# The last batch of a fused recurrence and mixture-of-experts kernel: both experts in token halves, with the gate and the output behind the second halves

## What is computed

```python
s0, s1, s2 = [_dense(x, share_wi[i], share_wo[i]) for i in range(3)]   # relu(x @ wi) @ wo, 256 -> 1024 -> 256
out_a = relu(x @ expert_wi[t]) @ expert_wo[t]         # t = type_idx of the batch
out_b = relu(x @ expert_wi[t + 1]) @ expert_wo[t + 1]
expert_out = out_a * wa + out_b * wb                  # wa, wb: softmax(gate_vecs / 0.1) of the type
gi = concatenate([expert_out[:, 0], s0[:, 0], s1[:, 0], s2[:, 0]])     # token 0 alone
g = softmax(relu(gi @ gate_w1) @ gate_w2)
out = expert_out * g[0] + s0 * g[1] + s1 * g[2] + s2 * g[3]
```

## Time and profile before

| | |
|---|---|
| median of 3 runs | 1095.56 us |
| the profiled execution's own time | 1094.21 us |
| its span, first to last instruction | 1092.3 us |
| TensorE busy | 98% of the span |
| VectorE busy | 70% |
| ScalarE busy | 37% |
| last matmul of the mixture starts | 1078.84 us |
| mean granted clock of TensorE | 0.998 of full speed |

### The profile page before, as it was taken

How to read it: one execution, slowest core, us unless ns; L and a number is a source line. 1 busy time by engine, 2 the same in 40 slices (tenths; PEclk the granted TensorE clock), 3 DMA queues, 4 the chain that set the end, 5 groups by cost and what they waited for, 6 DMA issues and landing times.

```text
span 1092.3 us, 12453 instructions
## 1 busy us (share of the span) xinstructions
PE 1074.0 (98%) x4754; PEld 862.7 (79%) x4754; DVE 764.0 (70%) x1245; ACT 398.9 (37%) x628; POOL 8.9 (1%) x20
## 2 busy tenths in 40 slices
PE   7899999999999999999999999999999999999998
PEld 5488777788887888878887888878888788888886
DVE  7979987499654995469753896549955598544234
ACT  6454445422334234332344223433234323322221
POOL 0000000000000000000000000000000000000000
PEclk9999999999999999999999999999999999999999
DMA  6359888676444564546544564545645465446550
GB/s 220 109 206 380 304 331 305 235 292 239 155 161 166 209 240 151 191 149 256 176 155 156 208 248 160 193 155 193 235 152 192 155 245 198 147 164 218 185 193 19
DMA packets 36476, 219.58 MB, mean 201 GB/s; under 512 B 4354, under 2 KB 4610, under 8 KB 14786
## 3 DMA queue, kind: packets, MB, share of 16 engines
q1 hardware_dynamic: 34114, 206.22, 52.4%
q0 software_dynamic: 2304, 12.58, 3.0%
HBM read 185.10 MB, written 33.69 MB: 200 GB/s over the span
## 4 chain that ended last, share of the span: by engine, by line
PE 87%; DVE 10%; issue 1%; ACT 1%; DMA 1%; SPq 0%; DVEq 0%
PE ps_up L581 13%; PE ps_up L582 13%; PE ps_up L583 13%; PE ps_down L582 12%; PE ps_down L583 12%; PE ps_down L581 12%; PE ps_aux L581 3%; PE ps_aux L583 3%; PE ps_aux L582 3%; DVE trace L1160 1%; DVE hid_lo L1063 1%; DVE trace L1191 1%; DVE wi L1055 1%; PE ps_aux L709 1%; DVE temporal L1200 1%
## 5 line engine op out<-in xcount | busy, mean ns | idle before, releaser
L1063 DVE SCALAR_TENSOR_TENSOR hid_lo<-ps_up,hid_hi 128x512 fp32r<-128x512 f32 x320 | 218.4, 685 | 272.5 <-ACT hid_hi L861 270.8
L861 ACT ACTIVATE hid_hi<-ps_up 128x512 fp32r<-128x512 f32 x320 | 191.2, 597 | 552.3 <-PE ps_up L583 551.7
L581 PE MATMUL ps_up<-x_hi_all,wi 128*128 128x512 f32 (+1 forms) x644 | 256.2, 398 | 0.1
L583 PE MATMUL ps_up<-x_hi_all,wi 128*128 128x512 f32 (+1 forms) x644 | 253.8, 394 | 0.0
L582 PE MATMUL ps_up<-x_lo_all,wi 128*128 128x512 f32 (+1 forms) x644 | 253.2, 393 | 0.0
L581 PE MATMUL ps_down<-hid_hi,wo 128*128 128x512 f32 x640 | 250.8, 392 | 1.4 <-DVE hid_lo L1063 1.0
L583 PE MATMUL ps_down<-hid_hi,wo 128*128 128x512 f32 x640 | 251.7, 393 | 0.0
L582 PE MATMUL ps_down<-hid_lo,wo 128*128 128x512 f32 x640 | 251.7, 393 | 0.0
L581 PEld LDWEIGHTS ps_down<-hid_hi,wo 128*128 128x128 f32 x640 | 120.2, 188 | 30.9 <-issue 2.6
L583 PEld LDWEIGHTS ps_up<-x_hi_all,wi 128*128 128x128 f32 x644 | 120.9, 188 | 29.1
L581 PEld LDWEIGHTS ps_up<-x_hi_all,wi 128*128 128x128 f32 x644 | 121.7, 189 | 27.6 <-DVE x_lo_all L1055 0.3
(11 more groups left out here) (202 smaller groups left out, 837.4 us busy)
## 6 DMA issues: line engine op xcount, KB each, us to landing
wi<-split_wi SPq DMA_DIRECT2D x70, 1024.0 KB, 4.8
wo<-split_wo SPq DMA_DIRECT2D x70, 1024.0 KB, 4.9
modb<-mod_scratch SPq DMA_DIRECT2D x28, 512.0 KB, 4.4
split_wi<-wi SPq DMA_DIRECT2D x10, 1024.0 KB, 6.6
split_wo<-wo SPq DMA_DIRECT2D x10, 1024.0 KB, 8.7
xt<-in_x SPq DMA_DIRECT2D x8, 512.0 KB, 6.3
split_wi<-ex POOLq DMA_DIRECT2D x4, 1024.0 KB, 7.9
split_wo<-ex POOLq DMA_DIRECT2D x4, 1024.0 KB, 6.6
```

Source lines behind the costliest of these rows:

```text
L581: pe.matmul(ps, w_hi, x_hi, start=start, stop=False)
L583: return pe.matmul(ps, w_lo, x_hi, start=False, stop=stop)
L861: act.activation(hid_hi[:, k % NU, :], ps_up[k % NU][:, :], ACT.Relu).then_inc(hid_hi_ready, 1)
L1063: dve.scalar_tensor_tensor(hid_lo[:, k % NU, :], ps_up[k % NU][:, :], 0.0, f32(hid_hi[:, k % NU, :]), ALU.max, ALU.subtract).then_inc(hid_ ...
```

## The change

In the last batch the slots of the two experts are split in token halves, in the order a, b, b, a: slots 24 to 31 are expert a on tokens 0 to 255, 32 to 39 expert b on the same, 40 to 47 expert b on tokens 256 to 511, 48 to 55 expert a on these. Expert b's weights stay in their buffers for 40 to 47; expert a's are loaded a second time, by eight DMAs of 512 KB that SyncE issues at slots 33, 34, 35 and 37, into tensors that the last batch no longer needs. Second-half expert b adds up in `ps_aux[1]`. A plan of its own, LAST_PLANS, places the gate and the mixing of this batch beside slots 40 to 55: the half-0 expert sum and the gate from slot 40 on, the mixing of half 0 at 44.5 to 46, the three shared terms of half 1 at 47.5 to 49.5, expert b at 50.5 and expert a behind slot 55, with one multiplication of VectorE each that reads the bank itself. Half 0 is stored at 47, half 1 at the end. The fillers and the diagonal matmuls are gone. The rows of `x2_hi`, `x2_lo`, `xg_hi` and `xg_lo` began 8, 16, 24 or 32 bytes behind the start of their tensor's 64-byte blocks, because of an edge of 2 elements ahead of each row; now they begin at multiples of 64 bytes (EDGE 2 becomes 16, and in `x2_hi` and `x2_lo` only the view that is read at an edge keeps one).

```diff
+LAST_PLANS = {
+    "sync": {47: ["store0"], 55.5: ["store1"]}, "tensor": {41.5: ["gate_hidden"]}, "scalar": {43: ["gate_exp"]},
+    "vector": {40: ["gate_part"], 42: ["gate_logits"], 43.5: ["gate_soft", "final_scale"],
+               44.5: ["final_early0"], 45: ["final_early1"], 45.5: ["final_early2"], 46: ["final_early3"],
+               47.5: ["final_late0"], 48.5: ["final_late1"], 49.5: ["final_late2"], 50.5: ["final_expert_b"],
+               55.5: ["final_expert_a"]}, "gpsimd": {},
+}
-EDGE = 2
-FINAL_OWN = P
+LAST_PASSES = ((0, slice(0, T)), (1, slice(0, T)), (2, slice(0, T)), (3, slice(0, HALF)), (4, slice(0, HALF)),
+               (4, slice(HALF, T)), (3, slice(HALF, T)))
+LAST_SLOTS = len(LAST_PASSES) * TPF
+AGAIN = LAST_SLOTS - TPF
+EDGE = 16
...
-        x2_hi_all = sb("x2_hi_all", [P, 2, CT, EDGE + T], F32R)
+        x2_hi_all = sb("x2_hi_all", [P, 2 * CT * T + CT * EDGE], F32R)
...
-                for k in range(SLOTS):
+                for k in range(LAST_SLOTS if last else SLOTS):
+                    if k == SLOTS:
+                        p = ending
...
+        again_wi = [(xg_hi, xg_lo), (ct_hi[:, :, :], ct_lo[:, :, :])]
+        again_wo = [(wc_hi[:, 0:UT * E], wc_lo[:, 0:UT * E]),
+                    tuple(t[:, 0, :, :].rearrange("p c t -> p (c t)") for t in (x2_hi, x2_lo))]
...
+                if last and k in (33, 34):
+                    load_again_wi(k - 33)
+                if last and k in (35, 37):
+                    load_again_wo((k - 35) // 2)
+                if last and k >= SLOTS:
+                    return
...
+                elif step in ("store0", "store1"):
+                    h = int(step[-1])
+                    sp.wait_ge(final_mixed[h], (NS + 1 + h) * CT)
+                    sp.dma_start(out[f].rearrange("p (c t) -> p c t", c=CT)[:, :, half(h)], x2[:, p.f_parity, :, half(h)])\
+                        .then_inc(last_stored[h], 16)
...
+                if j == 0 and at >= AGAIN:
+                    pe.wait_ge(again_loaded[u % 2], 64)
...
+                    if at == AGAIN:
+                        pe.wait_ge(experts_ready, b * 2 + 1 + c)
+                    start, stop = k % TPF == 0, k % TPF == TPF - 1
+                    bank = ps_down[c][:, tokens]
+                    if SLOTS <= at < AGAIN:
+                        bank = ps_aux[1][:, c * HALF:(c + 1) * HALF]
+                        start, stop = start and c == 0, stop and c == CT - 1
...
-            fill("mix", ps_aux[1])
-            pe.wait_ge(experts_ready, B * 2)
-            for at, i in enumerate(MIX_ORDER):
-                pe.wait_ge(final_diag, at + 1)
-                mm = pe.matmul(ps_aux[1][:, FINAL_OWN:T], final_gates[:, i * P:(i + 1) * P],
-                               y[:, y_at(i, (B - 1) % 2), 1, FINAL_OWN:T], start=(at == 0), stop=(at == 3))
-            mm.then_inc(final_sum, 1)
...
+            def final_add(h, at, parity, part, scale):
+
+                for c in range(CT):
+                    if at:
+                        dve.wait_ge(final_mixed[h], 2 * at - 1 + c)
+                    dve.scalar_tensor_tensor(x2[:, parity, c, half(h)], part(c), scale, x2[:, parity, c, half(h)],
+                                             ALU.mult, ALU.add).then_inc(final_mixed[h], 1)
...
+                elif step == "final_expert_a":
+                    dve.wait_ge(down_done, (B - 1) * SLOTS + LAST_SLOTS)
+                    final_add(1, NS + 1, parity, lambda c: ps_down[c][:, half(1)], final_w[:, 0:1])
...
                 elif step == "gate_part":
                     if final(f):
-                        dve.wait_ge(first_token, 2)
-                    else:
-                        dve.wait_ge(experts_ready, f * 2 + 2)
+                        add_expert_b(f, half(0), experts_ready)
+                    dve.wait_ge(experts_ready, f * 2 + 2)
```

More of the change, by code:

```diff
@@ L374, in drive, with run @@
         def drive(eng, mixture, beside):
-            def alone(p, slots):
-                for k in slots:
-                    for s in [*p.steps(eng, k), *p.steps(eng, k + 0.5)]:
-                        beside(s, k, p)
-            def run(b, parity, p, last):
-                for k in range(SLOTS):
+            def run(b, parity, p, last, ending=None):
+                for k in range(LAST_SLOTS if last else SLOTS):
+                    if k == SLOTS:
+                        p = ending
                     for s in p.steps(eng, k):
@@ L396, in drive, with slot_of @@
             last = Period(None, B - 2, None, 0, [first.uses[m] + (B - 2) * uses[m] for m in range(2)])
-            run(B - 1, 1, last, True)
-            yield "mixture ends"
             after = [first.uses[m] + (B - 2) * uses[m] + last.uses[m] for m in range(2)]
-            alone(Period(None, B - 1, None, 1, after), range(SLOTS))
+            run(B - 1, 1, last, True, Period(None, B - 1, None, 1, after, LAST_PLANS))
+        def slot_of(k, last):
+            if last:
+                ffn, tokens = LAST_PASSES[k // TPF]
+                return ffn * TPF + k % TPF, tokens
+            return k, slice(0, T)
+        again_wi = [(xg_hi, xg_lo), (ct_hi[:, :, :], ct_lo[:, :, :])]
+        again_wo = [(wc_hi[:, 0:UT * E], wc_lo[:, 0:UT * E]),
+                    tuple(t[:, 0, :, :].rearrange("p c t -> p (c t)") for t in (x2_hi, x2_lo))]
         block = ctx.enter_context(nc.Block())
@@ L486, in load_wo, with load_again_wi, load_again_wo @@
                 sp.dma_start(f32(wo[:, buf, :, :]).rearrange("p s f -> p (s f)"), source).then_inc(wo_landed[buf], 16)
+            def load_again_wi(half):
+                source = split_wi[bass.ds(expert["now"] + NS, 1), half].rearrange("o p (s c f) -> (o p) s c f", s=2, c=CT)
+                for part, place in enumerate(again_wi[half]):
+                    sp.dma_start(f32(place), source[:, part, :, :]).then_inc(again_loaded[half], 16)
+            def load_again_wo(half):
+                source = split_wo[bass.ds(expert["now"] + NS, 1), half].rearrange("o p (s f) -> (o p) s f", s=2)
+                for part, place in enumerate(again_wo[half]):
+                    sp.dma_start(f32(place), source[:, part, :]).then_inc(again_loaded[half], 16)
             def load_x(m):
@@ L569, in _ @@
             load_raw_wo(2)
-            for _ in drive("sync", mixture, beside):
-                pass
+            drive("sync", mixture, beside)
             sp.wait_ge(out_stored, (B - 1) * 16)
-            for c in range(CT):
-                sp.wait_ge(last_stored[c], 16)
+            for h in range(2):
+                sp.wait_ge(last_stored[h], 16)
         @block.tensor
@@ L583, in product, with up @@
                 return pe.matmul(ps, w_lo, x_hi, start=False, stop=stop)
-            def up(b, k, parity, tokens=slice(0, T), done=True):
+            def up(b, at, parity, tokens=None, done=True, last=False):
+                k, part = slot_of(at, last)
+                tokens = tokens or part
                 u, j = k // UT, k % UT
@@ L601, in up, with down @@
                     mm.then_inc(up_done, 1)
-            def down(b, k):
+            def down(b, at, last=False):
+                k, tokens = slot_of(at, last)
                 u, j = k // UT, k % UT
@@ L627, in mixture @@
                     pe.wait_ge(open_soma1, CT)
-                if k + LAG < SLOTS:
-                    up(b, k + LAG, parity)
+                if k + LAG < (LAST_SLOTS if last else SLOTS):
+                    up(b, k + LAG, parity, last=last)
                 elif not last:
                     up(b + 1, k + LAG - SLOTS, 1 - parity)
-                down(b, k)
+                down(b, k, last)
             def modulation(ps):
@@ L853, in tile_round, with relu @@
                 hi(ex[:, j % 2, 0, :].bitcast(F32R), ex[:, j % 2, 1, :]).then_inc(ex_hi_ready, 1)
-            def relu(b, k):
+            def relu(b, k, last=False):
+                tokens = slot_of(k, last)[1]
                 act.wait_ge(up_done, b * SLOTS + (k + 1))
@@ L1043, in _ @@
             relu(0, 1)
-            for _ in drive("scalar", mixture, beside):
-                pass
-            act.wait_ge(gate_soft, B * 6)
-            for i in MIX_ORDER:
-                act.activation(final_gates[:, i * P:(i + 1) * P], ident[:, :], ACT.Copy, scale=g[:, i:i + 1])\
-                    .then_inc(final_diag, 1)
+            drive("scalar", mixture, beside)
         @block.vector
@@ L1492, in _ @@
             wi_rest(1)
-            way = drive("vector", mixture, beside)
-            next(way)
-            add_expert_b(B - 1, slice(0, 1), first_token)
-            for _ in way:
-                pass
+            drive("vector", mixture, beside)
         @block.gpsimd
```

125 lines of the change are left out of this document (60 added, 65 removed).

## The result

| | before | after |
|---|---|---|
| median | 1095.55 us (4 runs, 1094.97 to 1095.74) | 1081.79 us (4 runs, 1081.22 to 1082.73) |
| the profiled execution's own time | 1094.21 us | 1081.45 us |
| its span | 1092.3 us | 1079.6 us |
| granted clock | 0.998 | 0.998 |

The mechanism forecast is there, and a second one, priced at nothing, adds two thirds as much.

A forecast was written before the change was run, and what follows sets the result against it. TensorE, busy 98% of the span at full clock, was taken as the bound, plus a long end. Terms -9.6 + 0.9 + 0.45 + 1.1 + 0.1 = -7.05 us took 1095.56 to 1088.5 us, range 1085.2 to 1091.6.

The forecast's parts named there:

- The new end: Behind slot 55's last matmul only drain, two adds and one store remain: 3.65 us against 13.2, saving 9.6.
- More matmuls: Last batch's experts: 384 matmuls of 256 columns replace 192 of 512, costing +0.9 us (0.6 to 1.5).
- Weight loads: Experts' weight loads double but overlap each other and the matmuls; nothing added beyond the 0.118 us spacing.
- The gate product: Last batch's gate product now stands between slots on TensorE: +0.45 us, upper bound 0.70.
- Stalls: TensorE waits for VectorE or ScalarE in the last batch, at slots 24, 32, 31/34 and 40 to 48: +1.1 us (0.4 to 3.0).
- Loads: Last weight units, asked for at double pace, may land late: +0.1 us (0 to 0.6); second loading of expert a free.
- Aligned rows: Rows starting at multiples of 64 bytes, touching every up of all batches: taken as 0 us, bounds -4.8 and +1.
- The row chosen as the arbiter: Profile row of a projection with aligned inputs: 1.40 us for six matmuls, just as the unaligned up, so no gain.
- 10 ns less, 15 at most: A down's time against an up's 1.40 us; if due to rows, up to 4.8 us gain over 320 groups.
- Rival 2: Row alignment matters in all batches: ups fall to the downs' pace, 4.8 us less, 1083.7 us; chance 0.15.
- Its sign: Slots at 2.77 us or less in batches 1 to 6 would mean that the rows count.
- The other rivals: Include VectorE bound beside halves (1091.0, chance 0.14), expert a late (1100, 0.04), weight loads standing alone (about 1125, 0.01).

The follow-up runs named there:

- `no_second_load`: Kernel after without the eight DMAs that load expert a again and the wait for them; slots 48 to 55 use expert b's weights: 1082.55 us, ratio 0.9888.
- `rows_only`: Kernel before with only the new aligned rows of the x2 and xg tensors, last batch unsplit: 1089.60 us, ratio 0.9952.
- the map: Separate program with only the matmul, relu slot pattern, operand starts moved singly or together: 1360 ns per six with nothing moved, 1394 for ups with high input moved 64 bytes.
- `match128`: Kernel after with x2_hi and x2_lo both starting at 128 modulo 256 bytes, like weights and hidden; four small tensors moved behind: 1075.22 us, ratio 0.9823.
- `both192`: Kernel after with x2_hi and x2_lo both starting at 192 modulo 256 bytes, unlike weights and hidden: 1083.80 us, ratio 0.9900.

## Why the prediction was wrong

Point by point, by the steps of the text:

- **The new end**: right in what is left; the forecast was 0.35 short. Counted from 0.12 behind the last matmul's start, 1075.61, to 1079.6 are 4.0 us against 3.65. The adds took 0.88 as forecast. The store is the difference: issued in 0.53 us instead of 0.35, and from the start of the issue to the end of the span 2.9 instead of 2.51, within the 3.2 kept as a bound for its shorter pieces.
- **More matmuls**: +0.9 forecast. What is left of the measured -7.42 when the end (-9.2), the waits and the gate product are taken out is +0.8. This is a remainder; the spacing itself, 0.118 at the median of the halves, is as forecast.
- **Weight loads**: as forecast, hidden at 256 columns too.
- **The gate product**: +0.43 against +0.45.
- **Stalls**: 0.56 against 1.1. Slot 24 cost 0.38 (0.3 forecast), slot 32 0.18 (0.05), slots 31/34 and 47/48 nothing (0.25 and 0.5). At slot 48 the low part was there 12.2 us behind down(39), forecast 12.85: a chain of some ten estimates ended 0.6 us too late, which was enough to make the 0.5 us of waiting that is not there. So -7.42 against -7.05 is nearer than its parts: the end gave 0.4 less than forecast, and the stalls took 0.5 less.
- **Loads**: 0, as forecast within 0.1, and the second loading free (`no_second_load`).
- **Aligned rows**: "I take 0 (bounds -4.8 and +1), by the row that differs in nothing but alignment and weights". This is the step that failed. Rows alone give -5.2 us (`rows_only`), so even the bound was a little narrow. With this term at -5.2 in place of 0 the same sum gives 1083.3, 1.5 us from the measured median.

Three things were wrong in it. The row chosen as the arbiter, was said to differ in nothing but alignment and weights. The runs show that the weights' own place, relative to the input, is just what counts: those inputs are aligned but do not share their start modulo 256 bytes with their weights, and by the rule that is why they are slow, like the unaligned ups; the same projection, as well aligned, is faster in `rows_only` (2.76 against 2.80 us for its 12). It spoke neither for nor against the rows. And the bound was set by the idea that only ups can gain; the map shows downs paced by where the neighbouring ups' inputs lie (moving only the ups' high input by 64 bytes takes the downs from 1360 to 1393). And the "10 ns less, 15 at most" came of an up in batch 6, an even one, taken from a slot of batch 7, an odd one. By the medians a down is 30 ns shorter than an up in even batches and 8 in odd ones, which is 19 on average and already more than that at most.

What the trace before held against the step and was not read: the same code had ups of 1405 and 1397 and downs of 1375 and 1389 ns in even and odd batches, and of what TensorE reads in a slot nothing differs between these but the half of `x2_hi` and `x2_lo`, so the offset of its rows. That was the experiment, already made in the profile. Rival 2 ("the rows matter", 1083.7) was the case that came, given 0.15, and the parity spoke for more. Its sign came too, a slot of 2.76 us in batches 1 to 6. Its mechanism did not: the ups did not fall to the pace of the downs (1391 against 1375), and the downs of the odd batches fell as well (1389 to 1375). The other rivals did not come: no wait of VectorE's between slots 44 and 52, expert a in time, loads overlapped.

## What to carry to other kernels

When a change touches something whose price no single row shows, look for a variation of it that the kernel already makes, by batch parity or buffer number, and compare medians over all of it, before taking one pair of rows as the judge. In a kernel bound by fp32r matmuls over 512 columns, try to lay out weights, inputs and hidden tensors so that all begin at the same place modulo 256 bytes; here that is worth 1.2% and costs 288 bytes of padding per partition (the 60 and 12 elements in `match128`). And after TensorE's pace has changed, read the waits again: the engine that was just in time is then late.

## What the runs showed of the hardware that was not expected

- The start of the operands against one another, with a period of 256 bytes, moves the spacing of fp32r matmuls over 512 columns between 227 and 240 ns, with all other engines at rest as well. A common start at 8 or 16 bytes beside a multiple of 32 costs too (1387 and 1380 per six against 1360). By which mechanism stays open: no run here tells one from another, and for starts that do not match the rule has no price (the kernel after, with 64 and 192, has 1391 and 1375, `both192` 1384 and 1389).
- At 256 columns the matched placement does not help: in `match128` the halves' matmuls start every 120 ns at the median, in the kernel after every 118, and the stretch from slot 23 to the end is 54.8 us against 54.3.
- A store of 256 KB in pieces of 1 KB took 0.53 us to issue at the end of the kernel after (0.54 in three other programs), in pieces of 2 KB 0.35 before.
- The opening comes out anywhere from 66.5 to 67.9 us, though its code is the same. One execution of each program was profiled, so whether the program decides it or chance stayed open; it is why single medians here should not be read closer than 1 us without the trace.
